# Edge convolutions of a four-layer graph kernel: one-hot picks summed in PSUM in two halves, maximum reading PSUM

## What is computed

```python
def _egnn_conv(x, src, dst, edge_attr, W_msg, W_edge, W_root, b):
    msg = x[src] @ W_msg + edge_attr @ W_edge
    agg = jax.ops.segment_max(msg, dst, num_segments=x.shape[0])
    agg = jnp.where(jnp.isneginf(agg), 0.0, agg)
    return agg + x @ W_root + b
...
c1 = jax.nn.leaky_relu(_egnn_conv(X, src, dst, edge_attr, W1_msg, W1_edge, W1_root, b1))
c2 = jax.nn.leaky_relu(_egnn_conv(c1, src, dst, edge_attr, W2_msg, W2_edge, W2_root, b2))
```

## Time and profile before

| | us |
|---|---|
| median of the timed runs | 2674.3 (2672.07 to 2676.32) |
| span of the profiled execution, first to last instruction | 2462.7 |
| median less that span, outside the instructions | 211.6 |
| busy in that span: TensorE | 2054.2 (83%) |
| VectorE | 1627.3 (66%) |
| GpSimd | 1245.4 (51%) |
| ScalarE | 874.7 (36%) |

### The profile page before, as it was taken

The page is one execution under the profiler, slowest core; times in us unless marked ns, Lnnn a source line. Parts: engine busy times, 40 slices in busy tenths (PEclk is TensorE's granted clock), DMA queues, the critical chain, the costliest instruction groups (busy, mean ns, idle before and its releaser), DMA issues. The chain is left out here.

```text
span 2462.7 us, 56144 instructions
## 1 busy us (share of the span) xinstructions
PE 2054.2 (83%) x21375; PEld 1842.5 (75%) x21375; DVE 1627.3 (66%) x4661; ACT 874.7 (36%) x1203; POOL 1245.4 (51%) x973
## 2 busy tenths in 40 slices
PE   5294539999999999999978859969999969999972
PEld 4142229999999999999977724459989958899872
DVE  6897996555555555555745640077888857888877
ACT  0195530000000000000012100049999918999950
POOL 0380018777778777774000000007777764777763
PEclk9995559999999999999988879969999968999985
DMA  3397002232322223231000059524445423454531
GB/s 135 85 385 266 1 4 22 22 32 22 32 22 22 22 23 32 22 32 22 18 7 2 1 219 355 194 58 125 146 142 165 122 86 101 141 166 127 162 117 40
DMA packets 150939, 227.56 MB, mean 92 GB/s; under 512 B 87649, under 2 KB 109825, under 8 KB 147106
## 3 DMA queue, kind: packets, MB, share of 16 engines
q1 hardware_dynamic: 70994, 186.72, 21.0%
q0 software_dynamic: 74688, 28.51, 11.9%
q10 hardware_dynamic: 5008, 9.07, 1.2%
HBM read 123.37 MB, written 100.84 MB: 91 GB/s over the span
## 5 line engine op out<-in xcount | busy, mean ns | idle before, releaser
L587 PE MATMUL ps<-parts,at 128*128 128x192 f16 x11250 | 960.4, 249 | 52.1 <-DVEq L686 23.5
L587 PEld LDWEIGHTS ps<-parts,at 128*128 128x128 f16 x11250 | 947.0, 99 | 59.8 <-issue 54.3
L1379 POOL DMA_INDIRECT messages_c<-y_table,srci_sb x504 | 509.6, 1011 | 389.3 <-DMA y_table<-ytab 236.4
L628 POOL DMA_INDIRECT weight_matrix<-w,place x392 | 611.9, 1561 | 168.3 <-issue 95.6
L1588 PE MATMUL ps<-yparts,source_onehots_c 128*128 128x192 f16 x7000 | 618.0, 248 | 35.0 <-ACT picked_pairs_c L1419 24.1
L1588 PEld LDWEIGHTS ps<-yparts,source_onehots_c 128*128 128x128 f16 x7000 | 574.2, 98 | 63.0 <-ACT picked_pairs_c L1419 50.3
L707 DVE SCALAR_TENSOR_TENSOR t<-ps,coef,g 128x96 f32<-128x96 f32 x400 | 126.9, 317 | 280.0 <-PE ps L587 278.8
L1407 ACT ACTIVATE source_gaps_c<-sources_spread,unshift 128x1280 f16<-128x1280 f16 x216 | 295.0, 1366 | 19.6 <-ACT source_onehots_c L1410 10.4
L656 ACT ACTIVATE ea_limbs<-ea_in,ea_scale 128x392 f16<-128x392 f32 x32 | 19.9, 621 | 792.5 <-DMA ea_in<-in_eaT 767.3
L1410 ACT ACTIVATE source_onehots_c<-source_gaps_c 128x1280 f16<-128x1280 f16 x216 | 274.4, 1270 | 6.9
L1462 DVE TENSOR_SCALAR source_onehots_c<-sources_spread,shift 128x1280 f16<-128x1280 f16 x484 | 270.4, 568 | 0.4
(11 more groups left out here) (360 smaller groups left out, 1449.7 us busy)
## 6 DMA issues: line engine op xcount, KB each, us to landing
weight_matrix<-blank SPq DMA_DIRECT2D x27, 1600.0 KB
weights<-weight_matrix SPq DMA_DIRECT2D x27, 1600.0 KB, 10.0
run_max<-messages_c SPq DMA_DIRECT2D x28, 960.0 KB
ea_c<-edge_limbs SPq DMA_DIRECT2D x28, 896.0 KB
edge_limbs<-ea_limbs SPq DMA_DIRECT2D x128, 98.0 KB
run_max<-messages_c SPq DMA_DIRECT2D x28, 384.0 KB, 4.0
sources_spread<-sources_by_tile ACTq DMA_DIRECT2D x26, 320.0 KB, 3.3
messages_c<-y_table,srci_sb POOLq DMA_INDIRECT x504, 2.6
```

What stands on the lines that cost most here:

```text
L587: mm = nc.tensor.matmul(m.ps[:, bank, 0:2 * D], m.at[:, s, blk * P:(blk + 1) * P], parts[:, s, :], start=(s == 0), stop=(s == NB - 1))
L628: nc.gpsimd.indirect_dma_start(cells, bass.IndirectOffsetOnAxis(m.place[:, t:t + 1], 0), m.w[:, t:t + 1], None, compute_op=ALU.add).then_i ...
L1379: nc.gpsimd.indirect_dma_start(msg[:, k % 2, j, :], None, d.yt, bass.IndirectOffsetOnAxis(m.srci[:, k * TURN + j:k * TURN + j + 1], 0)).th ...
```

## The change

The high and the low half of a pick become two products of 96 columns into the same 96 PSUM columns, so that PSUM adds them. A turn's 10 picked tiles then need 960 columns, two banks of five tiles (`SHARE`); odd and even turns have two banks each, and the edge terms four banks in place of three. The maximum of the first ten tiles reads its new row from PSUM. The bank copies (`take_rows`), the buffer `pairs` and the additions (`add_pairs`) are gone, with the semaphores `picked` and `paired`. VectorE waits for `closed`, once for five tiles; TensorE's first pick for turn k+1 waits until the ten maxima of turn k-1 have run (`ran`).

```diff
@@ -60,8 +60,9 @@
 XSCALE = 1024.0
 TN = T // TURN
 PICKS = 10
-PBANKS = PICKS // 2
-EBANKS = 8 - PBANKS
+SHARE = 5
+PBANKS = PICKS // SHARE
+EBANKS = 8 - 2 * PBANKS
 PK = PICKS * P
 EGROUPS = [(a, min(5, TURN - a)) for a in range(PICKS, TURN, 5)]
 NEG = len(EGROUPS)
@@ -1293,7 +1294,7 @@
         parts, scl, un = m.yparts, m.scl[:, layer:layer + 1], m.un[:, layer:layer + 1]
         ea = sb("ea", [LIMBS * DE, 2, TURN, P], F16)
         wl, wrest = sb("w_limbs", [LIMBS * DE, D], F16), sb("w_rest", [LIMBS * DE, D], F32)
-        msg, pairs = sb("messages", [P, 2, TURN, D], F32), sb("picked_pairs", [P, PICKS, 2, D], F32)
+        msg = sb("messages", [P, 2, TURN, D], F32)
         carT, carr, lastT = sb("carT", [D, P], F32), sb("carr", [P, D], F32), sb("lastT", [D, P], F32)
         hot = sb("source_onehots", [P, NB, PK], F16)
         after = carver(hot[:])
@@ -1306,8 +1307,7 @@
         got = [[sem(f"rows_{side}_{g}_gathered") for g in range(NEG)] for side in "ab"]
         srcl = m.srcl[layer]
         hotv, hota, gapd = sem("onehots_by_vector"), sem("onehots_by_scalar"), sem("gaps")
-        used, closed, picked = sem("onehots_used"), sem("picked_terms_added"), sem("rows_picked")
-        paired, seeded = sem("pairs_added"), sem("first_maximum_set")
+        used, closed, seeded = sem("onehots_used"), sem("picked_terms_added"), sem("first_maximum_set")
         terms, added, ran = sem("edge_terms"), sem("edge_terms_added"), sem("running_max")
         rst = [[sem(f"run_{side}_{h}_stored") for h in range(2)] for side in "ab"]
         lt, sc, ct, cc = sem("last_turned"), sem("carries"), sem("carry_turned"), sem("carry_copied")
@@ -1317,6 +1317,11 @@
         spread, ends, seld = sem("streams_spread"), sem("streams_in_rows"), sem("selector_made")
         b = c.enter_context(nc.Block())
         by_vector, by_scalar = len(BY_DVE), len(BY_ACT)
+
+        def picked_row(odd, i):
+
+            return m.ps[:, PBANKS * odd + i // SHARE, i % SHARE * D:(i % SHARE + 1) * D]
+
         more_by_vector = len(DVE_FIRST) - by_vector
 
         def made_by_scalar(k, b):
@@ -1410,22 +1415,12 @@
                     nc.scalar.activation(hot[:, b, :], gap[:], ACT.Relu, bias=1.0, scale=-1.0).then_inc(hota, 1)
                     a_.wait_ge(hota, n)
 
-            def take_rows(k):
-
-                for i in range(PBANKS):
-                    a_.wait_ge(closed, PBANKS * k + i + 1)
-                    if k >= 1:
-                        a_.wait_ge(paired, PBANKS * (k - 1) + i + 1)
-                    nc.scalar.activation(pairs[:, 2 * i:2 * i + 2, :, :].rearrange("p i a f -> p (i a f)"),
-                                         m.ps[:, i, 0:4 * D], ACT.Copy).then_inc(picked, 1)
-
             low = [b for b in BY_ACT if b < SPLIT_B]
             high = [b for b in BY_ACT if b >= SPLIT_B]
             onehots(0, ACT_FIRST)
             a_.wait_ge(hotv, len(DVE_FIRST))
             load_sources(2)
             onehots(1, low)
-            take_rows(0)
             for k in range(TN):
                 if k + 1 < TN:
                     onehots(k + 1, high)
@@ -1435,8 +1430,6 @@
                         a_.wait_ge(hotv, by_vector * (k + 2) + more_by_vector)
                         load_sources(k + 3)
                     onehots(k + 2, low)
-                if k + 1 < TN:
-                    take_rows(k + 1)
             if layer == 0:
                 a_.wait_ge(hotv, by_vector * TN + more_by_vector)
                 for k in range(2):
@@ -1476,19 +1469,13 @@
             onehots(1, low)
             v.wait_ge(seeded, 1)
 
-            def add_pairs(k, i):
-
-                v.wait_ge(picked, PBANKS * k + i + 1)
-                nc.vector.tensor_tensor(msg[:, k % 2, 2 * i:2 * i + 2, :], pairs[:, 2 * i:2 * i + 2, 0, :],
-                                        pairs[:, 2 * i:2 * i + 2, 1, :], ALU.add).then_inc(paired, 1)
-
             def add_terms(k, e):
 
                 a, n = EGROUPS[e]
                 v.wait_ge(terms, NEG * k + e + 1)
                 v.wait_ge(got[k % 2][e], 16 * n * (k // 2 + 1))
                 nc.vector.tensor_tensor(msg[:, k % 2, a:a + n, :], msg[:, k % 2, a:a + n, :],
-                                        blocks_of(m.ps[:, PBANKS + e % EBANKS, 0:n * D]),
+                                        blocks_of(m.ps[:, 2 * PBANKS + e % EBANKS, 0:n * D]),
                                         ALU.add).then_inc(added, 1)
 
             for k in range(TN):
@@ -1498,9 +1485,8 @@
                     v.wait_ge(rst[k % 2][0], 16 * (k // 2))
                 for j in range(TURN):
                     if j < PICKS:
-                        if j % 2 == 0:
-                            add_pairs(k, j // 2)
-                            v.wait_ge(paired, PBANKS * k + j // 2 + 1)
+                        if j % SHARE == 0:
+                            v.wait_ge(closed, PBANKS * k + j // SHARE + 1)
                     elif j in ESTART:
                         add_terms(k, ESTART[j])
                         v.wait_ge(added, NEG * k + ESTART[j] + 1)
@@ -1508,8 +1494,9 @@
 
                         v.wait_ge(ran, TURN * k + j)
                     prev = msg[:, k % 2, j - 1, :] if j else msg[:, 1 - k % 2, TURN - 1, :]
+                    row = picked_row(k % 2, j) if j < PICKS else msg[:, k % 2, j, :]
                     nc.vector.scalar_tensor_tensor(msg[:, k % 2, j, :], prev, m.brk[:, TURN * k + j:TURN * k + j + 1],
-                                                   msg[:, k % 2, j, :], ALU.add, ALU.max).then_inc(ran, 1)
+                                                   row, ALU.add, ALU.max).then_inc(ran, 1)
                     for n, x in enumerate(made):
                         if n * TURN // len(made) == j:
                             onehots(x[0], [x[1]])
@@ -1570,7 +1557,7 @@
 
         @b.tensor
         def _(pe):
-            def pick(k, odd, half, first, b):
+            def pick(k, odd, first, b, k_before):
 
 
                 if first and b in ACT_FIRST:
@@ -1581,22 +1568,22 @@
                     pe.wait_ge(hota, made_by_scalar(k, b))
                 else:
                     pe.wait_ge(hotv, made_by_vector(k, b))
+                if b == 0 and k_before is not None:
+                    pe.wait_ge(ran, TURN * k_before + PICKS)
                 for i in range(PICKS):
-                    if b == 0 and not first and i % 2 == 0:
-                        pe.wait_ge(picked, PBANKS * k + (i // 2 + 1 - PBANKS))
-                    at = 2 * D * (i % 2)
-                    mm = nc.tensor.matmul(m.ps[:, i // 2, at:at + 2 * D], hot[:, b, i * P:(i + 1) * P], parts[:, b, :],
-                                          start=(b == 0 and i % 2 == 0), stop=False, skip_group_check=True)
+                    for h in range(2):
+                        mm = nc.tensor.matmul(picked_row(odd, i), hot[:, b, i * P:(i + 1) * P], parts[:, b, h * D:(h + 1) * D],
+                                              start=(b == 0 and i % SHARE == 0 and h == 0), stop=False,
+                                              skip_group_check=True)
                 mm.then_inc(used, 1)
 
             def close(k, odd, half):
 
                 pe.wait_ge(eal[odd], 16 * half + 16)
                 for i in range(PICKS):
-                    at = 2 * D * (i % 2)
-                    mm = nc.tensor.matmul(m.ps[:, i // 2, at:at + D], ea[:, odd, i, :], wl[:], start=False,
-                                          stop=(i % 2 == 1), skip_group_check=True)
-                    if i % 2:
+                    mm = nc.tensor.matmul(picked_row(odd, i), ea[:, odd, i, :], wl[:], start=False,
+                                          stop=(i % SHARE == SHARE - 1), skip_group_check=True)
+                    if i % SHARE == SHARE - 1:
                         mm.then_inc(closed, 1)
 
             def edge_terms(k, odd, half, first, e):
@@ -1608,7 +1595,7 @@
                 elif not first:
                     pe.wait_ge(added, NEG * k + (LAST_USE[e] + 1 - NEG))
                 for j in range(n):
-                    mm = nc.tensor.matmul(m.ps[:, PBANKS + e % EBANKS, j * D:(j + 1) * D], ea[:, odd, a + j, :], wl[:],
+                    mm = nc.tensor.matmul(m.ps[:, 2 * PBANKS + e % EBANKS, j * D:(j + 1) * D], ea[:, odd, a + j, :], wl[:],
                                           start=True, stop=True)
                 mm.then_inc(terms, 1)
 
@@ -1620,13 +1607,13 @@
                     if more:
                         upto = -(-(e + 1) * NB // NEG)
                         for b in range(done, upto):
-                            pick(k + 1, 1 - odd, half + odd, False, b)
+                            pick(k + 1, 1 - odd, False, b, None if first else k - 1)
                         done = upto
                 if more:
                     close(k + 1, 1 - odd, half + odd)
 
             for b in range(NB):
-                pick(0, 0, 0, True, b)
+                pick(0, 0, True, b, None)
             pe.wait_ge(wscaled, 1)
             close(0, 0, 0)
```

## The result

| kernel | first chips, us | other chips, us |
|---|---|---|
| before | 2673.2 (2670.6 to 2676.3) | 2462.8 (2462.0 to 2466.1) |
| changed | 2734.05 (2731.9 to 2735.6) | 2492.4 (2491.4 to 2494.7) |
| ratio, 95% interval | 1.0229 (1.0214 to 1.0243) | 1.0115 (1.0098 to 1.0132) |

A forecast was written before the change was run, and what follows sets the result against it. Gathers were taken to bound both convolutions at 23.4 to 23.7 us a turn, ending 3.7 and 2.8 us earlier: 6.5, rounded to 7, off 2674.3 gives 2667 us; range 2642 to 2682, likeliest case 2660 to 2669.

The forecast's parts named there:

- Picks in two halves: TensorE, edge convolutions: 250 products of 192 columns become 500 of 96 at 42.5 ns, a turn of 22.4 us.
- the other bound: TensorE's halved picks at the slowest short f16 pair, 66 ns each, which would make a turn 34.8 us.
- The base: Timed median 2674.3 us against the profiled span of 2462.7; the 211.6 us outside the span were taken as unchanged.
- Bank copies and pair additions dropped: ScalarE from 23.90 to 22.03 us a turn; TensorE loses 1.04 and 0.8 us of delay; VectorE saves 1.8 us.
- TensorE bounds: Sign against the forecast: VectorE waiting for closing products all along, where over 50 us of waiting for gathered rows was expected.
- Gathers: GpSimd's 18 row gathers a turn bound both convolutions; their lengthening falls from 17.7 and 15.6 us to 14 each.
- Rival 3: Gathers lose their lengthening almost wholly and fall into step with TensorE: 30 us less, 2644 us; chance 0.16.
- the 51 and 15.1 us: Gathers on GpSimd: 51 of 191 lengthened ones have a pair addition in them, with 15.1 of 33.3 us.
- the Trainium skill's rule on SBUF: VectorE against GpSimd: by it pair additions would cost gathers nothing, lengthening would stay near 33 us, no change of time.
- Maximum from PSUM: VectorE's maxima reading PSUM: 317 ns in the aggregation against 323 now, so no change.
- Banks of two turns: TensorE's first pick of turn k+1 waits for maxima of turn k-1, which ran some 15 us before.
- Rival 5: Load and product of 96 columns sustained above 45.4 ns make TensorE slower; at 66 ns 2957 us; chance 0.06.

The follow-up runs named there:

- written-out kernel: TensorE's loop over the turns written out, against the changed kernel: 2438.4 us against 2492.4 on the other chips, 2701.0 on the first kind.
- with 8 picks: 8 picked and 20 gathered tiles a turn in place of 10 and 18, against the changed kernel: 2512.9 us, 1.0213 of the kernel before.
- the long loop of the kernel before: TensorE's loop of four turns, two passes, in place of two turns, five passes, against the kernel before: 2467.7 us, one run.

## Why the prediction was wrong

**The step that failed** is in *Picks in two halves*: "At that pace a turn is 528 x 0.0425 = 22.4 us, 0.6 more work than now". On the other chips the pace was right to the tenth: 42 to 43 ns from start to start, 22.4 us a turn wherever there is no branch. The 66 ns of the other bound was far off, and products in a row into the same columns cost nothing. (The 81 ns for a load and product of 128 columns in the Trainium skill, "TensorE: Matmul & The Clock Gate", section Back-to-back issue gap, isn't borne out at 96 columns; 128 were not run.) What the step leaves out is the instructions. It counted products as time and not as code, and put the supply of instructions at nothing without a reason; doubling 250 products adds 1000 instructions to a loop of two turns, which takes it from 1180 to 2174, past a point between 1530 and 1774 from which the branch back has to fetch. On the other chips that costs TensorE (27.05 - 22.5) x 2 = 9 us at each of the eight branches back: in the pass shown 7.3 us in the two gaps and the rest in the pace at the lower clock. These are 73 us in all. Part is hidden, because in the written-out kernel the convolution ends with the gathers, 14.6 us behind TensorE: 54 us are left.

The Trainium skill has a rule for this that I had not weighed: "Runtime: NRT & Kernel Launch", section Instruction fetch mechanics, states that TensorE's instruction RAM holds 2048 instructions, is refilled in blocks of 16 KiB or 256 instructions, and that a taken branch to a target outside a window of two blocks stalls on a fetch. The trace agrees with that on the stall (a branch of 4.9 us, then 2.6 us idle) and on the block (16 KB packets). On the limit it agrees with neither figure: bodies of 1180 and 1530, more than two blocks, stayed, and one of 1774, below 2048, was fetched again. The trace of before had the warning as well: its instruction queue is silent inside the loop and busy outside, so the loop was living on what stays. The queue also brings 11 packets a pass where the written-out kernel needs 33 for eight turns, 8.25 for two, so part of what it brings isn't used.

**The base** was wrong too: "the 211.6 us outside the span don't change". They were a difference between the two kinds of chips. On the first kind the turn is 29.4 us, not 23.9, and what the earlier trace rows show of who is late doesn't hold there: the changed kernel without its loop is even 0.57% slower than the one before, with turns of 30.4 us. So on the chips of the timed runs the forecast of 7 us less fails twice, by the 52 us of the loop and by some 22 that stay unexplained. An unexplained 8% between a profile's span and the timed runs should have been a doubt about the profile, not a constant.

**Point by point**, on the other chips, written out, where the loop is out of the way:

- Bank copies and pair additions dropped: right, and neither ScalarE nor VectorE sets the turn. But VectorE's idle went elsewhere than I said. In ten turns of 263 us 30.0 us of it end on the closing products and only 2.5, once, on gathered rows; these come late in the last turn (3.12 us above). The prediction had named that as its sign of being wrong, "TensorE bounds":

```profile
DVE messages_c L1498 <- PE ps L1584: 30.0, 10, 3.5
...
DVE messages_c L1477 <- DMA messages_c<-y_table,srci_sb: 2.5, 1, 2.5
```

- So TensorE sets the turn at 22.5 us and the gathers only the end; I had the gathers for both, at 23.4 to 23.7.
- Gathers: busy 242.4 and 242.6 us a convolution against 255.9 and 253.7, a lengthening of 4.3 and 4.5 us, where I took 14. Rival 3, gathers and products in step, was the right one for this kernel: from the first gather to the last 317.9 us in place of 331.4. I gave 7 us for it all and 30 by that rival; it is 24.4 (2462.8 - 2438.4). The working behind the 14 was weak: counted again over the trace of before, pair additions run beside 111 of the long gathers, with 20.0 us of their lengthening, and start inside 44 of them, with 10.3; the 51 and 15.1 us lie between and hang on how "in" is meant. And the Trainium skill's rule on SBUF that the prediction quotes was applied wrongly: a gather has `srci_sb`, an SBUF tile, among its inputs, so by that rule a pair addition can block it. The fall of the lengthening agrees with that, but no run drops the additions alone.
- Maximum from PSUM: on the first chip 310 ns from PSUM against 317 from SBUF, no dearer; forecast nothing.
- Banks of two turns: no wait of TensorE's picks for the maxima shows in the written-out kernel, as said.
- Rival 5, slower pairs, had the right sign and the wrong mechanism. TensorE came to more than 23.9 us a turn at 42.5 ns a pair; agreement with that rival would have been luck.

So the chance of slower, 0.14, came from the rivals that I had, and none of them was about the code or the clock.

## What to carry to other kernels

Count the instructions of a loop body on each engine before an edit that multiplies them: here up to 1530 on TensorE stayed and 1774 didn't, and 2174 cost TensorE 9 us at each branch back. The instruction queue's packets inside a loop of the profile tell on which side one is, and writing the loop out cost nothing here, where the stream kept up with a packet every 5.4 us. A stall of TensorE costs more than its length: behind one of 4.3 us the granted clock was at 0.50. If a profile's span and the timed runs differ by per cents, take a second profile before building a sum on the first; and judge a change whose sum hangs on who is late on both kinds of chips (here, written out, 0.990 on one and 1.006 on the other).

## What the runs showed of the hardware

- A load and product of 96 f16 columns keeps 42.5 ns for a whole turn of 528, half of the 82.5 ns of one with 192 columns: between these two the price goes by columns.
- A branch back over a body that doesn't stay took TensorE 3.3 to 5.7 us, with an instruction packet arriving in it. In the changed kernel a second gap follows (2.2 to 2.6 us idle in the passes shown), with its own packet; with 8 picks, in the first convolution, and in the long loop of the kernel before none does. A hint removed most of the first stall alone.
- Behind these stalls the granted clock was at 0.50 for 7 to 10 us in the first convolution, and 39 products took 78 ns each.
- Written-out code for TensorE at 42.5 ns a pair took 16 KB of instructions every 5.4 us, at turns of 22.4 us.
- The kernel before ran at two times 9% apart on chips of two kinds, whose nature isn't known. All of it lies behind the first picks of the edge convolutions, which start at 1641 to 1646 us on both. On the slower kind VectorE began on TensorE's signal some 0.6 us later, and signalling once in five blocks cost 182 us in place of nothing.
